# Two changes of order in a four-stage image kernel: where the scan makes and spreads delta*u, and when attention sums its products

## What is computed

```python
# attention: em = positional + image embedding; unfold = 9 shifted copies
feature_score = jnp.einsum('bckhw,bchw->bkhw', unfold3x3(em), em)
comp_score = sigmoid(jnp.einsum('bckhw,c->bkhw', unfold3x3(inp), w_comp))
out = jnp.einsum('bckhw,bkhw->bchw', unfold3x3(inp), comp_score * feature_score)
# mamba, two layers, 16 states n, 128 inner channels d, over l = 65536 pixels
delta = softplus(xdbl[..., :dt_rank] @ dt_w.T + dt_b)
dA  = exp(einsum('bld,dn->bldn', delta, A))
dBu = einsum('bld,bln,bld->bldn', delta, Bm, u)
h = dA_t * h + dBu_t            # for each pixel, in order
y = einsum('bdn,bn->bd', h, C_t)
```

## Time and profile before

| | |
|---|---|
| time, median of 3 runs | 19584.36 us (19577.68 to 19585.76) |
| the profiled execution | 19583.1 us, of it 19581.3 in the span from the first instruction to the last |
| busy in the span | DVE 18051.3 (92%), Pool 17267.8 (88%), PE 12771.9 (65%), ACT 11274.2 (58%) |
| attention's 64 full steps | 389.3 to 1433.5 us of the span |
| scan, 256 tasks | about 1500 to 15740 us |
| the FFT and DCT layers | 15740 us to the end |
| DVE's scans (line 1279) | 4096 of 2.33 to 2.35 us, 9527 us |
| DVE's products in the scan (1273) | 3072 of 1.23 us, 3784 us |
| Pool's h*c (1323) | 4096 of 2.36 us, 9605 us |

### The profile page before, as it was taken

How to read it: one execution, slowest core, us unless ns; L and a number is a source line. 1 busy time by engine, 2 the same in 40 slices (tenths; PEclk the granted TensorE clock), 3 DMA queues, 4 the chain that set the end, 5 groups by cost and what they waited for, 6 DMA issues and landing times. The chain is left out here.

```text
span 19581.3 us, 147925 instructions
## 1 busy us (share of the span) xinstructions
PE 12771.9 (65%) x45790; PEld 4695.5 (24%) x45790; DVE 18051.3 (92%) x11642; ACT 11274.2 (58%) x12399; POOL 17267.8 (88%) x7417
## 2 busy tenths in 40 slices
PE   4775666666666666666666666666666668888885
PEld 2221111111111111111111111111111134444444
DVE  5888999999999999999999999999999979999996
ACT  1115666666666666666666666666666646666663
POOL 3888999999999999999999999999999969999991
PEclk8997777777777777777777777777777789999997
DMA  3325555555555555555555555555555511111114
GB/s 123 104 97 132 134 133 138 135 137 135 132 134 137 139 134 131 134 138 137 135 133 134 136 138 135 133 133 135 138 135 135 130 34 33 33 31 28 33 29 142
DMA packets 616198, 2249.23 MB, mean 115 GB/s; under 512 B 74881, under 2 KB 92147, under 8 KB 591091
## 3 DMA queue, kind: packets, MB, share of 16 engines
q1 hardware_dynamic: 610146, 2232.63, 44.0%
q10 hardware_dynamic: 5265, 7.14, 0.1%
HBM read 990.77 MB, written 174.96 MB: 60 GB/s over the span
## 5 line engine op out<-in xcount | busy, mean ns | idle before, releaser
L1323 POOL TENSOR_TENSOR h<-h,c_bc 128x1024 f32<-128x1024 f32 x4096 | 9604.8, 2360 | 994.7 <-DVE h L1279 993.6
L1279 DVE TENSOR_TENSOR_SCAN h<-da,state,px 128x1024 f32<-128x1024 f32 x3072 | 7210.3, 2347 | 109.7
L1150 ACT ACTIVATE da<-d_bc,a_neg 128x1024 f32<-128x1024 f32 x3072 | 3493.0, 1145 | 2648.8 <-DVE h L1279 2611.5
L1004 PE MATMUL py<-h,ysel 128*32 128x512 f32 x16384 | 2496.2, 737 | 2817.9 <-POOL h L1323 2816.1
L1273 DVE TENSOR_TENSOR px<-px,du_bc 128x1024 f32<-128x1024 f32 x3072 | 3783.7, 1232 | 515.6 <-PE px L990 232.3
L1909 POOL TENSOR_TENSOR acc<-acc,ta 128x1024 f32<-128x1024 f32 (+1 forms) x1040 | 2426.2, 2342 | 396.7 <-DVE acc L1809 293.5
L1315 POOL TENSOR_TENSOR xs<-du_bc,b_bc 128x1024 f32<-128x1024 f32 x1024 | 2412.1, 2356 | 0.0
L1279 DVE TENSOR_TENSOR_SCAN h<-px,state,xs 128x1024 f32<-128x1024 f32 x1024 | 2317.0, 2326 | 0.0
L990 PE MATMUL px<-cf,bsel 32*128 32x512 f32 x3072 | 1336.6, 957 | 1180.3 <-DVE h L1279 1180.3
L1809 DVE SCALAR_TENSOR_TENSOR p_c<-zb,w_dw,p_c 128x1024 f32<-128x1024 f32 (+1 forms) x1560 | 1987.1, 1274 | 43.7 <-PE p_c L1581 11.2
L1150 ACT ACTIVATE px<-d_bc,a_neg 128x1024 f32<-128x1024 f32 x1024 | 1144.2, 1117 | 905.5 <-DVE h L1279 891.4
(11 more groups left out here) (219 smaller groups left out, 19351.9 us busy)
## 6 DMA issues: line engine op xcount, KB each, us to landing
d_bc<-delta SPq DMA_DIRECT2D x1024, 512.0 KB, 8.5
du_bc<-du SPq DMA_DIRECT2D x1024, 512.0 KB, 8.9
c_bc<-c_rows_dram SPq DMA_DIRECT2D x1024, 512.0 KB, 6.1
b_bc<-c_rows_dram SPq DMA_DIRECT2D x256, 512.0 KB, 8.1
hx<-x_dram SPq DMA_DIRECT2D x252, 256.5 KB, 6.3
st_x<-in_x_dram SPq DMA_DIRECT2D x32, 1024.0 KB, 4.9
ax<-in_x_dram SPq DMA_DIRECT2D x64, 512.0 KB, 3.5
xr<-x_dram SPq DMA_DIRECT2D x64, 512.0 KB, 6.1
```

The lines of the kernel that those rows point to most:

```text
L1004: last = nc.tensor.matmul(py[32 * j:32 * j + 32, cut], ysel[:, :], h[:, (4 * q + j) % 8, cut], start=False, stop=(q == Q - 1))
L1150: nc.scalar.activation(out[:, :], d_bc[:, n % J, :], ACT.Exp, scale=a_neg[t.l][:, n:n + 1]).then_inc(da_done, 1)
L1279: nc.vector.tensor_tensor_scan(h[:, n % 8, PAD:T + PAD], a[:, :], x[:, :], state[:, 2 * t.l + t.b, n:n + 1], ALU.mult, ALU.add).then_inc(s ...
L1323: nc.gpsimd.tensor_tensor(out=h[:, n % 8, 0:T], in0=h[:, n % 8, PAD:T + PAD], in1=c_bc[q % 2][:, :], op=ALU.mult).then_inc(m2_done, 1)
```

## The change

In the scan `DU_AT` goes from 6 to 10: Pool makes the next task's delta*u behind its product 10. In `spread_first` the first spread of delta*u is issued ahead of the last spread of delta. In attention TensorE's sum of tile 4 moves from behind spread 8 to behind spread 0 of the next step, the sum of tile 6 from behind spread 2 to behind spread 3, and the sum of tile 0 from behind spread 7 to behind spread 8. The amount of work is the same.

```diff
                     halves(p_f[(s.par + k) % 2], fsel[:, k, :], fb[s.par]).then_inc(f_ps, 1)
-                    if k == 2 and s.from_(1):
+                    if k == 0 and s.from_(1):
+                        add(s.other(-1), 4)
+                    if k == 3 and s.from_(1):
                         add(s.other(-1), 6)
                     if k == 5 and not s.last and not s.other(1).last:
                         score(s.other(1))
-                    if k == 7:
+                    if k == 8:
                         add(s, 0)
-                    if k == 8:
-                        add(s, 4)
 
             score(Step(0))
             run(step)(pe)
+            add(Step(NK), 4)
             add(Step(NK), 6)
...
-        OUT_AT, DU_AT, ZN_AT = 0, 6, 13
+        OUT_AT, DU_AT, ZN_AT = 0, 10, 13
...
                 for j in range(J - 1):
                     spread_delta(t, j)
                 spread_b(t)
+                spread_du(t, 0)
                 spread_delta(t, J - 1)
-                spread_du(t, 0)
                 spread_c(t, 0)
                 for j in range(1, J):
                     spread_du(t, j)
```

## The result

The changed kernel takes **19281.5 us** (median; 19279.9 to 19282.8) against 19581.0 before, ratio 0.9848, interval 0.9832 to 0.9864. The forecast was 19310, 0.986. The profiled execution took 19279.9 us, 303.2 less than that of before.

What follows compares the result with a forecast made beforehand. The prediction took VectorE's own work plus its gaps, with Pool close behind, to bound scan and attention. From 19584 us, -206 for the scan and -68 for attention gave 19310 us; own ends 19235 and 19365, range extended to 19430.

Steps and rivals of the forecast that it cites:

- What bounds the kernel: Scan and attention: the time is VectorE's own work plus the gaps in it, with Pool close behind.
- Step 12's waits: Scan: VectorE's waits at step 12 for TensorE's B spread all go as product 7 comes earlier, -128 us.
- step 4: Scan: VectorE's waits there for TensorE's B spread stay, 0.71 each, 91 us in all, costing 7 us more.
- The du waits: Scan: VectorE's waits for delta*u spreads go as SP's line starts earlier, -90 us, some 5 us of lateness left.
- The order of du 0 and delta 3: SP's queue in the scan: du 0 ahead of delta 3 by itself changes one place in the line; no size given.
- Scan, -206 us: Scan total: -128 - 90 + 5 + 7 = -206 us, 0.8 a task.
- Attention, -68 us: Attention: new order of sums leaves one 0.8 us gap, steps 16.3 to 15.3 us with three in five cold.
- Rival (a): Scan: only one of the two gains comes, step 12 or du waits; 19390 to 19426, say 19410 us; chance 0.10.
- (b): Attention gives nothing, cold in every step, the scan as forecast; 19378 us; chance 0.08.
- (d): The change does nothing, or TensorE's waits move to the next instruction; 19584 us, give or take 30; chance 0.04.
- Rival (c): Scan: delta*u, head of SP's queue, over 3.9 us late; one us beyond costs 256 us, 19644; chance 0.04.
- The ends: Forecast's own ends: 19235 (attention -108, step 4's waits halved) and 19365 (attention -20, 30 of the scan lost).

Runs made afterwards that it cites:

- Run 11: The changed kernel with SP's last c spread of a task waiting for Pool's product 8 instead of 7; 19458.1 us.
- runs 3 and 4: The kernel before with one scan edit each: 3, only delta*u behind product 10, 19373.0 us; 4, only du 0 issued ahead of delta 3, 19572.8 us.
- run 2: The kernel before with both scan edits, attention as before; 19377.5 us.
- Run 7: The changed kernel with TensorE's idle time behind attention spreads 6 and 7 filled by extra products that add(0) overwrites; 19255.6 us.
- run 1: The kernel before with only attention's new order of sums, the scan as before; 19477.4 us.
- Run 5: The changed kernel with Pool's delta*u one product later, behind product 11 (`DU_AT` 11); 19387.2 us.
- run 6: The changed kernel with Pool's delta*u behind product 12 (`DU_AT` 12); 20394.7 us.
- run 9: The changed kernel with attention's idle TensorE time filled by extra products, plus the sum of tile 6 moved behind spread 4; 19284.8 us.

## Why the prediction was right, point by point

- **What bounds the kernel.** Right: the change took nothing from VectorE's work and everything from its gaps.
- **Step 12's waits, -128 us.** Right. They are gone; step 4 kept 127 waits of 0.7, 89.1 us against 91 worked out. Add_y in the task shown still ran at a granted clock of 0.50 (1.2 GHz), and the spread behind it, at 1.00 (2.4 GHz), ended 1.2 before the earliest start instead of 0.2. In 136 of the 256 tasks the spread took the 2.1 us of the lower level, and no task waited for it, so the small margin held.
- **The du waits, -90 us, 5 left.** Right. Beyond the wait ahead of the first task, 44.1 - 32.8 = 11.3 us are left in 13 waits, 1.4 of dispatch in it: 10 instead of 5. The first du spread went 11.7 us ahead of its task, 12.0 worked out. Run 11 shows the chain.
- **The order of du 0 and delta 3.** I gave it no term of its own, and runs 3 and 4 show that it has none: 0.04% alone, nothing on top. All 3328 spreads of the scan landed in the order of issue, in the kernel before as in the changed one, a median of 2.5 us apart, so the swap only moved the wait within the task. The Trainium skill's rule that completion is not first in, first out for an issuing engine ("DMA: Bandwidth & Descriptors", Queues, rings and completion order) does not show in these transfers, all of one size.
- **Scan, -206 us.** Right: 200.5 from first to last product, and 205 in the time of run 2.
- **Attention, -68 us.** Right in its mechanism, and its size was off: it gave 98. The warm step was 14.6 and measured 14.45 (the gap at product 4 is 0.6, not 0.8: the sum of tile 6 began at 2.8 and took 1.90, not 1.98). That is 10 us. The share of cold steps, those with a stretch at the granted clock of 0.50, was mis-sized more, by 21 us. I took three in five from the kernel before, at 1.1 each; it is one stretch in three steps, which costs 0.15 in its own step and 0.84 in the next (14.45, 14.60, 15.29), 0.33 on average instead of 0.66. Run 7, which takes the clock's part away, gives 14.45. The new order leaves TensorE less idle time: its gaps in the 64 steps fell from 234.9 to 167.2 us, those over 0.8 us from 190 to 88. That this is why the clock fell less often was not tried by itself, and the three moves of sums were not tried one by one.
- **Rival (a)**, one of two gains: it did not come about here, though run 11 shows what it would be. **(b)**, attention gives nothing: fell with run 1. **(d)**, the change does nothing: fell with the result.
- **Rival (c)**, Pool's delta*u as the head of SP's queue: the mechanism is real, and its point and price were both wrong. I put the point 3.9 us behind where delta*u ends and the price at one us a task for each us beyond it, counting du 0 alone. Run 5 costs 0.4 a task at 2.3 us, and run 6 4.3, some 5.6 us late. What counts most is du 1, the third spread behind the one that waits; its margin was 1.5 us. In run 6 du 0 adds some 0.8 us a task.
- **The ends.** With the terms named, the forecast's own ends (45 us for half of step 4's waits) are 19584 - 206 - 108 - 45 = 19225 and 19584 - 176 - 20 = 19388, not 19235 and 19365. The measured time is far from both.

## What to carry to other kernels

Look for the instruction on which several queues hang, here one product on Pool with a transfer line and a TensorE queue behind it, and move what stands in front of it, if that has slack; the order inside the queue behind it was worth nothing.
When a queue head waits, look at every transfer in the burst behind it: the price here was set by the one with the least margin (du 1), not by the head's own margin and not by the last in line (du 3, which no product waited for); and where two waits lie in one period, taking one away brings the other forward.
Closing a visible gap can uncover a longer wait elsewhere: run 9 closed one of 0.6 us a step, met a sum at the lower clock, and lost 29 us.

## What the runs showed of the hardware

- Products that nobody needs made TensorE faster where it counts: in run 7 the window's granted clock went from 0.95 to 1.00 and the stage from 946.1 to 924.6 us.
- The issue of a 512 KB spread took SP 0.55 us where it was short (median), and much longer in a burst. In the kernel before, 1702 of the 3328 spread issues took over 1.5 us (median 2.6, at most 5.3), and 1550 of these 1702 ended with exactly two earlier spreads still on their way. So a burst of spreads keeps SP itself busy, and what SP has to do behind it waits as well.
- The spreads of the scan landed in the order in which SP issued them, all 3328 of them, in both kernels.
